# Graph attention and gated experts on one Trainium2 core: the softmax by one exponential with the true row maximum, and the gate's running sum on VectorE

## The chip, the core and the metric

The kernel runs on one core of one Trainium2 chip. The time is device time in microseconds (us), the median of the runs; lower is better. Everything is computed in float32, in matmuls either as float32 or as a sum of products of rounded halves.

## What is computed

Two layers in one kernel over 128 graphs of 128 nodes with 256 features. The first is graph attention; the second is a set of 8 expert networks (two hidden layers with batch norm and relu, one output layer), added up with a gate. Cut to what matters:

```python
# attention, on h = layernorm(x)
Wh = h @ W
e = s1[:, :, None] + s2[:, None, :]            # s1 = Wh @ a1, s2 = Wh @ a2
e = where(e > 0, e, 0.2 * e) + log(adj + 1e-6)
x = x + softmax(e, axis=-1) @ Wh
# experts, on x' = layernorm(x)
feat = mean(x', axis=0)                         # over the 128 graphs
w = softmax(feat @ Wr + br)                     # the gate, one row per node
x = x + sum over experts of w * (relu(bn(relu(bn(x' @ W1)) @ W2)) @ Wo + bo)
```

The logarithm is never taken: the kernel forms exp(leaky(s1+s2) - m) * (adj + 1e-6) and divides by the row's sum. Any m that is constant along a row gives the same softmax.

## The kernel before

The kernel has two blocks, one after the other. The first works through the attention, four graphs at a time (a group): G = 32 groups, tiles of 128 partitions (nodes) by GB = 4 graphs by 128 or 256 columns. Between the blocks the x after attention (x1) goes through DRAM. The second block runs the 8 experts over the 32 groups (tiles).

In the first block all engines run the same step function 34 times and more, each in its own instruction order, tied by semaphores. In step g, SyncE and the engines work at several groups at once: `ago(g, n)` is the group n steps back. In one step:

- TensorE (PE) first transposes p_sb of the group b = g-2 (`ps_pT`, L757), then broadcasts s2 of the group a = g-1 into `ps_s` (L765), then projects the first half of group g (L745), multiplies p by Wh for b (L784), projects the second half, and transposes the normalised x of g+1 (L797) once VectorE has read `ps_h` (the two share PSUM).
- VectorE (DVE), for a: row maximum of s2 out of `ps_s` (`s2max`, L620), three small steps on 128x4 tiles to the two biases of the exponentials (`neg_u` L623, `neg_m` L628, `exp_bias` L634 and L635), with the four statistics instructions of x of g+2 between them (L584). Since s1 + max(s2) bounds the row, the maximum needs only s2. Then the reciprocal of the row sums (L660), the aggregation of the statistics of g+2 (L598) and of x1 of g-3 (L603), x1 of b = PSUM times reciprocal plus residual (L676, four instructions), then for a the larger of the two exponentials (`e_max`, L687), times adjacency (`p_sb`, L694), the row sum (L701), and between them and behind them the statistics of x1 of b (L592, four).
- ScalarE (ACT): copies pT (L524), scales x1 of g-4, graphs 0 and 1, by its 1/std (`x1s_low`, L531), normalises x of g+1 (L514, four), takes two exponentials for each graph of a, of s1+s2 and of 0.2*(s1+s2) (L544 and L546, eight in all; exp of the leaky relu is the larger of them), then a rounding of expert weights (L558 or L562) and the copies of Wh (L567) and of the transposed x (L571).
- GpSimd (POOL): 1/std of x for g+2 by a power (L405 to L412), the sum of the gate over graphs 0 and 1 of g-4 (`acc[:, :HB]`, in the memory of `resb`, L444), the mean and 1/std of x1 of g-3 (L452 to L456), scaling (L462) and summing (L466) of graphs 2 and 3 of g-3, then the preparation of expert weights: in 16 steps either four sums (L472 to L479) or `wq_lo` (L484), in the next 8 `w_lo` (L489).

`acc` holds the sum over groups of x1/std, from which the gate's `feat` comes in the second block. The last two groups are added by `add_group` (L179): four instructions on DVE, x1 times a column of 1/std plus acc, 128x256 each.

The step for group a in DVE's order can't begin before `ps_s` is there, and `ps_s` stands in PE's queue behind the transposes of `p_sb` of the step before.

Of the kernel before, what the change touches and what calls it, by code (L numbers as in the profile page):

```python
# [38 lines left out]
def adj_ffn(nc, x, adj, gnn_w, gnn_a, wr, br, w1, b1, g1, be1, m1, v1, w2, b2, g2, be2, m2, v2, wo, bo, out):  # L39
# [17 lines left out]
    with ExitStack() as ctx:  # L57
# [3 lines left out]
        def sem(name, stack=ctx):  # L61
            return stack.enter_context(nc.semaphore(name))
# [122 lines left out]
        with ExitStack() as sa:  # L185
            def sba(name, shape, dt=F32):
                return sb(name, shape, dt, sa)
# [24 lines left out]
            s2max = sba("s2max", [P, GB])  # L212
            neg_u = sba("neg_u", [P, GB])
            neg_m = sba("neg_m", [P, GB])
            exp_bias = [sba(f"exp_bias{i}", [P, 2, GB]) for i in range(2)]
            e_sb = sba("e_sb", [P, 2, GB, N])
            e_max = sba("e_max", [P, GB, N])
# [7 lines left out]
            x1s_low = sba("x1s_low", [P, HB, D])  # L225
            x1s_high = sba("x1s_high", [P, HB, D])
# [38 lines left out]
            s2max_done = sem("s2max_done", sa)  # L265
            neg_u_done = sem("neg_u_done", sa)
            neg_m_done = sem("neg_m_done", sa)
            bias_done = sem("bias_done", sa)
            e_max_done = sem("e_max_done", sa)
# [13 lines left out]
            x1s_low_done = sem("x1s_low_done", sa)  # L283
            x1s_high_done = sem("x1s_high_done", sa)
            acc_low_done = sem("acc_low_done", sa)
            acc_high_done = sem("acc_high_done", sa)
# [6 lines left out]
            def num(g):  # L293
                return 2 * g[0] + g[1]
# [93 lines left out]
            def _(pool):  # L388
# [5 lines left out]
                nc.gpsimd.memset(acc[:, :, :], 0.0)  # L394
# [38 lines left out]
                def step(g, layer):  # L433
# [5 lines left out]
                    h = ago(g, 4)  # L439
                    if exists(h):  # L440

                        pool.wait_ge(x1s_low_done, num(h) + 1)
                        wait(pool, acc_low_done, num(h))
                        nc.gpsimd.tensor_tensor(acc[:, :HB, :], acc[:, :HB, :], x1s_low[:, :, :],  # L444
                                                ALU.add).then_inc(acc_low_done, 1)
                    t = ago(g, 3)
                    if exists(t) and not is_step(t, G - 1):

                        p = t[1]
                        pool.wait_ge(stats2_done, num(t) + 1)  # L450
                        wait(pool, rstd2_done, num(t))
                        nc.gpsimd.tensor_tensor(mean_all[:, num(t), :], mv2[p][:, :, 0], ones_cols[:, :], ALU.mult)  # L452
                        nc.gpsimd.tensor_tensor(ve2[:, :], mv2[p][:, :, 1], eps_cols[:, :],
                                                ALU.add).then_inc(ve2_done, 1)
                        pool.wait_ge(ve2_done, num(t) + 1)
                        nc.gpsimd.tensor_tensor(rstd_all[:, num(t), :], ve2[:, :], minus_half[:, 0:GB],  # L456
                                                ALU.pow).then_inc(rstd2_done, 1)
                        pool.wait_ge(rstd2_done, num(t) + 1)
                    if exists(t) and not is_step(t, G - 2) and not is_step(t, G - 1):

                        wait(pool, acc_high_done, num(t))
                        nc.gpsimd.tensor_tensor(x1s_high[:, :, :], x1[p][:, HB:, :],  # L462
                                                rstd_all[:, num(t), HB:, None].to_broadcast([P, HB, D]),
                                                ALU.mult).then_inc(x1s_high_done, 1)
                        pool.wait_ge(x1s_high_done, num(t) + 1)
                        nc.gpsimd.tensor_tensor(acc[:, HB:, :], acc[:, HB:, :], x1s_high[:, :, :],  # L466
                                                ALU.add).then_inc(acc_high_done, 1)
# [31 lines left out]
            def _(act):  # L499
# [18 lines left out]
                def step(g, layer):  # L518
# [6 lines left out]
                    t = ago(g, 4)  # L525
                    if exists(t):

                        act.wait_ge(rstd2_done, num(t) + 1)
                        wait(act, acc_low_done, num(t))
                        for b4 in range(HB):  # L530
                            last = nc.scalar.activation(x1s_low[:, b4, :], x1[t[1]][:, b4, :], ACT.Copy,  # L531
                                                        scale=rstd_all[:, num(t), b4:b4 + 1])
                        last.then_inc(x1s_low_done, 1)
# [3 lines left out]
                    a = ago(g, 1)  # L537
                    if exists(a):
                        r = a[1]
                        act.wait_ge(bias_done, num(a) + 1)  # L540
                        wait(act, e_max_done, num(a))

                        for b4 in range(GB):
                            nc.scalar.activation(e_sb[:, 0, b4, :], ps_s[:, b4, :], ACT.Exp,  # L544
                                                 bias=exp_bias[r][:, 0, b4:b4 + 1])
                            last = nc.scalar.activation(e_sb[:, 1, b4, :], ps_s[:, b4, :], ACT.Exp,  # L546
                                                        bias=exp_bias[r][:, 1, b4:b4 + 1], scale=SLOPE)
                        last.then_inc(e_done, 1)
# [29 lines left out]
            def _(dve):  # L578
# [27 lines left out]
                def step(g, layer):  # L606
# [10 lines left out]
                    if exists(a):  # L617

                        dve.wait_ge(s2b_ready, num(a) + 1)
                        nc.vector.tensor_reduce(s2max[:, :], ps_s[:, :, :], AX_X, ALU.max).then_inc(s2max_done, 1)  # L620
                        stats_part(0)
                        dve.wait_ge(s2max_done, num(a) + 1)
                        nc.vector.scalar_tensor_tensor(out=neg_u[:, :], in0=s2max[:, :], scalar=-1.0,  # L623
                                                       in1=wh[r][:, :, D], op0=ALU.mult,
                                                       op1=ALU.subtract).then_inc(neg_u_done, 1)
                        stats_part(1)
                        dve.wait_ge(neg_u_done, num(a) + 1)
                        nc.vector.scalar_tensor_tensor(out=neg_m[:, :], in0=neg_u[:, :], scalar=SLOPE,  # L628
                                                       in1=neg_u[:, :], op0=ALU.mult,
                                                       op1=ALU.min).then_inc(neg_m_done, 1)  # L630
                        stats_part(2)
                        dve.wait_ge(neg_m_done, num(a) + 1)
                        wait(dve, e_done, num(a) - 1)
                        nc.vector.tensor_tensor(exp_bias[r][:, 0, :], wh[r][:, :, D], neg_m[:, :], ALU.add)  # L634
                        nc.vector.scalar_tensor_tensor(out=exp_bias[r][:, 1, :], in0=wh[r][:, :, D], scalar=SLOPE,  # L635
                                                       in1=neg_m[:, :], op0=ALU.mult,
                                                       op1=ALU.add).then_inc(bias_done, 1)
                        stats_part(3)
                    else:
                        for b4 in range(GB):  # L640
                            stats_part(b4)
                    if is_step(g, G - 1):
                        dve.wait_ge(rstd2_done, 1)
                        tile_normalise(dve, 0, range(HB))
                        tile_normalise(dve, 0, range(HB, GB))
# [3 lines left out]

# [15 lines left out]
                    if exists(b):  # L665
# [5 lines left out]
                        wait(dve, x1s_low_done, num(b) - 1)  # L671
                        wait(dve, x1s_high_done, num(b) - 1)
# [10 lines left out]
                    if exists(a):  # L683
# [3 lines left out]
                        nc.vector.tensor_tensor(e_max[:, :, :], e_sb[:, 0, :, :], e_sb[:, 1, :, :],  # L687
                                                ALU.max).then_inc(e_max_done, 1)
                        if with_stats:
                            stats_2(b, 0)  # L690
                        dve.wait_ge(e_max_done, num(a) + 1)
# [3 lines left out]
                                                       in1=e_max[:, :, :], op0=ALU.add,  # L695
# [22 lines left out]
                dve.wait_ge(acc_low_done, G - 2)  # L718
                dve.wait_ge(acc_high_done, G - 2)
# [4 lines left out]
            def _(pe):  # L724
# [24 lines left out]
                def step(g, layer):  # L749
# [9 lines left out]
                    if exists(a):  # L759

                        pe.wait_ge(wh_copied, num(a) + 1)
                        wait(pe, e_done, num(a))
                        wait(pe, s2max_done, num(a))
# [537 lines left out]
```

## Time and profile before

| | us |
|---|---|
| median of 3 runs | 2500.86 |
| lowest, highest run | 2500.14, 2605.57 |
| the profiled execution | 2498.69 |
| its span | 2496.9 |
| busy in the span: PE, DVE, ACT, POOL | 2395.4, 1758.3, 1657.6, 520.9 |

The profiled execution is one of its own; its span is the time between the first and the last instruction. The row of busy tenths in 40 slices (62.4 us each) shows two parts: up to about 340 us DVE is at 9 tenths and PE at 7, and from about 400 us PE is at 9 and DVE at 6. In a row of the timeline, the first column is the start in us from the span's start, the second how long the instruction (or the merged run of xN instructions) lasted. An instruction's duration holds some 0.08 us that the next one on the same engine overlaps, so the pace is read from start to start.

### The profile page before, as it was taken

Reading aid. Unit: us, or ns where it says so; the run is one execution under the profiler, and the core shown is the slowest. Engines: PE = TensorE matmul, PEld = TensorE weight load, DVE = VectorE, ACT = ScalarE, POOL = GpSimd, SP = SyncE. Lnnn points to the kernel's source line nnn. Section 1 sums busy time; section 2 is a strip of 40 time slices with the busy share of each in tenths; the row PEclk is TensorE's granted clock in tenths of the full one; section 3 lists DMA queues with packets and bytes.
Section 4 is the critical chain, followed back from the end, with each engine's and each line's share of the span. In section 5 each row is a group of like instructions: output and inputs, shape, how many; then the busy total and the mean of one; then the engine's idle time right before and its main releaser. Section 6 shows DMA issues by size and latency. Waiting matters only on the chain.

```text
span 2496.9 us, 45276 instructions
## 1 busy us (share of the span) xinstructions
PE 2395.4 (96%) x16304; PEld 2208.3 (88%) x16304; DVE 1758.3 (70%) x2512; ACT 1657.6 (66%) x2526; POOL 520.9 (21%) x548
## 2 busy tenths in 40 slices
PE   7877769999999999999999999999999999999999
PEld 6666658999999999999999999999999999999998
DVE  6999966666666666666666666666666666666665
ACT  6777746666666666666666666666666666666665
POOL 5888852111111100110111111111111101110110
PEclk9999989999999999999999999999999999999999
DMA  5666620000000000000000000000000000000000
GB/s 183 197 191 193 199 95 26 27 26 25 25 25 25 25 25 25 23 19 18 15 25 25 25 25 25 25 25 25 25 25 25 25 25 25 22 20 18 16 18 26
DMA packets 91178, 116.16 MB, mean 47 GB/s; under 512 B 4700, under 2 KB 78856, under 8 KB 91144
## 3 DMA queue, kind: packets, MB, share of 16 engines
q1 hardware_dynamic: 91144, 115.73, 14.4%
q8 instruction: 19, 0.31, 0.1%
q14 instruction: 15, 0.12, 0.0%
HBM read 82.16 MB, written 33.55 MB: 46 GB/s over the span
## 4 chain that ended last, share of the span: by engine, by line
PE 84%; DVE 1%; ACT 0%; issue 0%; ACTq 0%; DVEq 0%
PE ps_y L1201 29%; PE ps_wide L171 29%; PE ps_wide L1183 26%; PE ps_t L132 1%; DVE h_lo L1088 0%; PE ps_y L1249 0%; DVE h L1095 0%; DVE z L1081 0%; ACT h_hi L990 0%; DVE x1t L124 0%; DVE feat_sum L1121 0%; ACT v L995 0%; DVE resb L179 0%; DVE z L1071 0%; DVE h_lo L1103 0%
## 5 line engine op out<-in xcount | busy, mean ns | idle before, releaser
L995 ACT ACTIVATE v<-ps_wide,bn_cols 128x256 f32<-128x256 f32 x768 | 434.3, 565 | 398.8 <-PE ps_wide L1183 271.5
L1003 ACT ACTIVATE h<-ps_wide,bn_cols 128x512 f32<-128x512 f32 x512 | 399.1, 780 | 327.3 <-PE ps_wide L171 327.2
L1201 PE MATMUL ps_y<-wo_lo,h_hi 128*128 128x256 f32 x2048 | 578.8, 283 | 0.0
L1201 PE MATMUL ps_y<-wo_hi,h_hi 128*128 128x256 f32 x2048 | 577.1, 282 | 1.6 <-DVE h_lo L1103 1.6
L1201 PE MATMUL ps_y<-wo_hi,h_lo 128*128 128x256 f32 x2048 | 578.3, 282 | 0.0
L1183 PE MATMUL ps_wide<-xq_hi,wq_hi 128*128 128x256 f32 x1792 | 505.5, 282 | 15.4 <-PEq L185 9.9
L1183 PE MATMUL ps_wide<-xq_lo,wq_hi 128*128 128x256 f32 x1792 | 509.2, 284 | 0.0
L1183 PE MATMUL ps_wide<-xq_hi,wq_lo 128*128 128x256 f32 x1792 | 506.6, 283 | 0.0
L1103 DVE TENSOR_TENSOR h_lo<-h,h_hi 128x1024 fp32r<-128x1024 f32 x256 | 318.3, 1243 | 242.2 <-ACT h_hi L1009 242.2
L1081 DVE SCALAR_TENSOR_TENSOR z<-ps_wide,bn_cols,v 128x512 f32<-128x512 f32 x256 | 192.4, 752 | 318.1 <-PE ps_wide L1183 318.1
L171 PE MATMUL ps_wide<-h_hi,w_hi 128*128 128x512 f32 x1024 | 404.0, 395 | 2.1 <-DVE h_lo L1088 2.1
L171 PE MATMUL ps_wide<-h_lo,w_hi 128*128 128x512 f32 x1024 | 405.7, 396 | 0.0
L171 PE MATMUL ps_wide<-h_hi,w_lo 128*128 128x512 f32 x1024 | 405.6, 396 | 0.0
L973 POOL TENSOR_TENSOR resb<-resb,bias_out 128x1024 f32<-128x1024 f32 x32 | 84.2, 2633 | 1535.8 <-DMA resb<-x_scratch 1535.8
L1088 DVE SCALAR_TENSOR_TENSOR h_lo<-z,h_hi 128x1024 fp32r<-128x1024 f32 x256 | 315.8, 1233 | 117.8 <-ACT h_hi L990 117.7
L1201 PEld LDWEIGHTS ps_y<-wo_hi,h_hi 128*128 128x128 f32 x2048 | 386.5, 189 | 1.9 <-DVE h_lo L1103 1.8
L1201 PEld LDWEIGHTS ps_y<-wo_hi,h_lo 128*128 128x128 f32 x2048 | 387.3, 189 | 0.0
L1201 PEld LDWEIGHTS ps_y<-wo_lo,h_hi 128*128 128x128 f32 x2048 | 386.4, 189 | 0.0
L1183 PEld LDWEIGHTS ps_wide<-xq_hi,wq_hi 128*128 128x128 f32 x1792 | 340.6, 190 | 28.0 <-issue 10.7
L1183 PEld LDWEIGHTS ps_wide<-xq_hi,wq_lo 128*128 128x128 f32 x1792 | 337.9, 189 | 10.0
L1183 PEld LDWEIGHTS ps_wide<-xq_lo,wq_hi 128*128 128x128 f32 x1792 | 339.5, 189 | 0.0
L1095 DVE TENSOR_TENSOR h<-h,w_bc 128x1024 f32<-128x1024 f32 x256 | 313.3, 1224 | 7.8 <-ACT w_bc L1037 4.9
(136 smaller groups left out, 3270.7 us busy)
## 6 DMA issues: line engine op xcount, KB each, us to landing
x_sb<-in_x SPq DMA_DIRECT2D x32, 512.0 KB, 3.5
res<-in_x SPq DMA_DIRECT2D x32, 512.0 KB, 4.5
x1t<-x_scratch SPq DMA_DIRECT2D x32, 512.0 KB, 3.3
resb<-x_scratch SPq DMA_DIRECT2D x32, 512.0 KB, 3.3
out<-resb SPq DMA_DIRECT2D x32, 512.0 KB, 3.0
adj_sb<-in_adj SPq DMA_DIRECT2D x32, 256.0 KB, 3.9
x_scratch<-h SPq DMA_DIRECT2D x16, 512.0 KB, 3.5
x_scratch<-w_bc SPq DMA_DIRECT2D x16, 512.0 KB, 3.0
```

The source lines that it names most:

```text
L132: last = nc.tensor.transpose(ps_x[:, c, b4 * N:(b4 + 1) * N], x1t[:, b4, c * P:(c + 1) * P], ident[:, :])
L171: mm = nc.tensor.matmul(acc_ps, w[:, i, c, cols], s[:, c, :], start=start and n == 0, stop=stop and n == len(terms) - 1)
L973: nc.gpsimd.tensor_tensor(resb[:, :, :], resb[:, :, :], bias_out[:, None, :].to_broadcast([P, GB, D]), ALU.add).then_inc(resb_done, 1)
L995: nc.scalar.activation(v[:, slot, :], ps_l1[:, 0, 0:H], ACT.Identity, bias=bn_cols[:, 1, cols], scale=bn_cols[:, 0, cols]).then_inc(done, 1)
L1003: nc.scalar.activation(h2[:, m, :], ps_l2[:, m, :], ACT.Relu, bias=bn_cols[:, 3, cols], scale=bn_cols[:, 2, cols]).then_inc(r2_done, 1)
L1081: nc.vector.scalar_tensor_tensor(out=z[:, 0, :], in0=ps_l1[:, 1, :], scalar=bn_cols[:, 0, C * e:C * e + 1], in1=v[:, 0:2, :].rearrange("p ...
L1088: nc.vector.scalar_tensor_tensor(out=h1_lo[:, :, :], in0=z[:, :, :], scalar=0.0, in1=h1_hi[:, :, :].bitcast(F32), op0=ALU.max, op1=ALU.sub ...
L1095: nc.vector.tensor_tensor(h2w[:, :, :].rearrange("p c (b n) -> p (c b) n", n=N), h2[:, :, :].rearrange("p c (b n) -> p (c b) n", n=N), w_b ...
L1103: nc.vector.tensor_tensor(h2_lo[p][:, :, :], h2w[:, :, :], h2_hi[p][:, :, :].bitcast(F32), ALU.subtract).then_inc(lo2_done, 1)
L1183: mm = nc.tensor.matmul(out_ps, w[:, e, q, :], x[:, q, :], start=start and n == 0, stop=stop and n == len(terms) - 1, skip_group_check=True)
L1201: mm = nc.tensor.matmul(ps_y[:, b4, :], h[:, c, cols], w[:, e, c, :], start=(e == 0 and k == 0 and b4 % per_bank == 0), stop=(e == E - 1 a ...
```

## The change

For each group the leaky relu is now computed itself. ScalarE writes s1+s2 from PSUM to SBUF (`s_sb`, Identity with s1 as bias, four instructions); DVE takes the larger of it and 0.2 times it (`l_sb`, one scalar_tensor_tensor 128x512) and its negated row maximum (`neg_m`, one reduction 128x512); ScalarE takes one exponential for each graph (four instead of eight), with `neg_m` as bias; `p_sb` reads it directly. `s2max`, `neg_u`, `exp_bias` and `e_max` are gone.

The gate's sum moves: the scaling on ScalarE (two instructions) and the scaling and both sums on GpSimd are gone; DVE does scale and add in four instructions, 128x256 each, for the group g-4, ahead of the reciprocal. The copy of the mean (`mean_all`) goes from GpSimd to ScalarE.

```diff
@@ GpSimd, step
-                    h = ago(g, 4)
-                        nc.gpsimd.tensor_tensor(acc[:, :HB, :], acc[:, :HB, :], x1s_low[:, :, :], ALU.add)
...
-                        nc.gpsimd.tensor_tensor(mean_all[:, num(t), :], mv2[p][:, :, 0], ones_cols[:, :], ALU.mult)
...
-                        nc.gpsimd.tensor_tensor(x1s_high[:, :, :], x1[p][:, HB:, :], rstd_all[...], ALU.mult)
-                        nc.gpsimd.tensor_tensor(acc[:, HB:, :], acc[:, HB:, :], x1s_high[:, :, :], ALU.add)
@@ ScalarE, step, behind the copy of pT
-                    t = ago(g, 4)
-                        for b4 in range(HB):
-                            last = nc.scalar.activation(x1s_low[:, b4, :], x1[t[1]][:, b4, :], ACT.Copy, scale=...)
+                    a = ago(g, 1)
+                        act.wait_ge(s2b_ready, num(a) + 1)
+                        for b4 in range(GB):
+                            last = nc.scalar.activation(s_sb[:, b4, :], ps_s[:, b4, :], ACT.Identity,
+                                                        bias=wh[r][:, b4, D:D + 1])
+                    t = ago(g, 3)
+                        nc.scalar.activation(mean_all[:, num(t), :], mv2[t[1]][:, :, 0], ACT.Copy)
@@ ScalarE, behind normalise(nxt)
-                        act.wait_ge(bias_done, num(a) + 1)
+                        act.wait_ge(neg_m_done, num(a) + 1)
                         for b4 in range(GB):
-                            nc.scalar.activation(e_sb[:, 0, b4, :], ps_s[:, b4, :], ACT.Exp, bias=...)
-                            last = nc.scalar.activation(e_sb[:, 1, b4, :], ps_s[:, b4, :], ACT.Exp, bias=..., scale=SLOPE)
+                            last = nc.scalar.activation(e_sb[:, b4, :], l_sb[:, b4, :], ACT.Exp,
+                                                        bias=neg_m[:, b4:b4 + 1])
@@ DVE, step
-                        (s2max, stats 0, neg_u, stats 1, neg_m, stats 2, exp_bias twice, stats 3)
+                        stats_part(0)
+                        stats_part(1)
+                        dve.wait_ge(s_done, num(a) + 1)
+                        nc.vector.scalar_tensor_tensor(out=l_sb[:, :, :], in0=s_sb[:, :, :], scalar=SLOPE,
+                                                       in1=s_sb[:, :, :], op0=ALU.mult, op1=ALU.max)
+                        stats_part(2)
+                        dve.wait_ge(l_done, num(a) + 1)
+                        nc.vector.tensor_reduce(neg_m[:, :], l_sb[:, :, :], AX_X, ALU.max, negate=True)
                         stats_part(3)
+                    h = ago(g, 4)
+                        for b4 in range(GB):
+                            last = nc.vector.scalar_tensor_tensor(out=acc[:, b4, :], in0=x1[h[1]][:, b4, :],
+                                                                  scalar=rstd_all[:, num(h), b4:b4 + 1],
+                                                                  in1=acc[:, b4, :], op0=ALU.mult, op1=ALU.add)
...
-                        nc.vector.tensor_tensor(e_max[:, :, :], e_sb[:, 0, :, :], e_sb[:, 1, :, :], ALU.max)
```

## Rows read from the trace of the kernel before

**Rows 1.** Busy time by stretch; after the width: PE, PEld, DVE, ACT, POOL, granted clock, DMA share, GB/s
```profile
90.00:110.00 20.00, 17.02 (x83) 14.59 (x83) 17.56 (x54) 15.17 (x34) 18.30 (x25) 0.83 0.63 197
110.00:230.00 120.00, 91.57 (x514) 76.61 (x513) 118.86 (x345) 93.06 (x206) 105.84 (x149) 1.00 0.63 195
...
310.00:350.00 40.00, 24.40 (x120) 20.61 (x120) 32.41 (x87) 19.73 (x49) 27.39 (x32) 0.86 0.33 109
...
400.00:2400.00 2000.00, 1999.19 (x14034) 1867.16 (x14033) 1355.90 (x1481) 1323.60 (x1846) 229.31 (x155) 1.00 0.07 23
```

**Rows 2.** Groups of DVE's, then POOL's instructions, 53 to 309 us: count | busy us, mean ns
```profile
L694 DVE SCALAR_TENSOR_TENSOR p_sb<-adj_sb,e_max 128x512 f32<-128x512 f32 x26 | 37.2, 1430 | 0.0
L628 DVE SCALAR_TENSOR_TENSOR neg_m<-neg_u 128x4 f32<-128x4 f32 x25 | 23.4, 934 | 0.0
...
L634 DVE TENSOR_TENSOR exp_bias<-wh,neg_m 128x4 f32<-128x4 f32 x25 | 20.9, 834 | 0.0
...
L701 DVE TENSOR_REDUCE rowsum<-p_sb 128x4 f32<-128x512 f32 x25 | 16.6, 663 | 0.0
...
L484 POOL TENSOR_TENSOR wq_lo<-w_stage,wq_hi 128x896 f32 x8 | 16.7, 2088 | 0.0
```

**Rows 3.** Timeline of DVE, one step with little work on POOL
```profile
39.48 0.69 DVE L620 TENSOR_REDUCE s2max<-ps_s 128x4 f32<-128x512 f32 x1
40.09 0.42 DVE L584 BATCH_NORM_STATS2 st<-x_sb 128x6 f32<-128x256 f32 x1
...
41.23 0.15 DVE L634 TENSOR_TENSOR exp_bias<-wh,neg_m 128x4 f32<-128x4 f32 x1
...
42.44 1.62 DVE L676 SCALAR_TENSOR_TENSOR w_bc<-ps_th,rinv,res 128x256 f32<-128x256 f32 x4
43.99 0.68 DVE L687 TENSOR_TENSOR e_max<-e_sb 128x512 f32<-128x512 f32 x1
44.59 0.42 DVE L592 BATCH_NORM_STATS2 st<-w_bc 128x6 f32<-128x256 f32 x1
44.92 0.67 DVE L694 SCALAR_TENSOR_TENSOR p_sb<-adj_sb,e_max 128x512 f32<-128x512 f32 x1
...
47.24 0.69 DVE L620 TENSOR_REDUCE s2max<-ps_s 128x4 f32<-128x512 f32 x1
```

**Rows 4.** Timeline of all engines, DVE and POOL in the middle of the stage
```profile
152.77 1.66 DVE L676 SCALAR_TENSOR_TENSOR h<-ps_th,rinv,res 128x256 f32<-128x256 f32 x4
...
154.36 1.80 POOL L444 TENSOR_TENSOR resb<-resb,x1s_low 128x512 f32<-128x512 f32 x1
...
155.28 1.42 DVE L694 SCALAR_TENSOR_TENSOR p_sb<-adj_sb,e_max 128x512 f32<-128x512 f32 x1
...
162.97 1.02 POOL L409 TENSOR_TENSOR rstd<-ve,minus_half 128x4 f32<-128x4 f32 x1
...
163.73 0.68 DVE L687 TENSOR_TENSOR e_max<-e_sb 128x512 f32<-128x512 f32 x1
```

**Rows 5.** The same timeline, PE and ACT
```profile
156.76 0.66 PE L757 MATMUL ps_pT<-ident,p_sb 128*128 128x128 f32 x4 [1.61 <-DVE p_sb L694]
...
157.25 1.06 PE L765 MATMUL ps_s<-ident,wh 128*128 128x128 f32 x8
...
161.22 0.37 ACT L544 ACTIVATE e_sb<-ps_s,exp_bias 128x128 f32<-128x128 f32 x1
161.49 0.36 ACT L546 ACTIVATE e_sb<-ps_s,exp_bias 128x128 f32<-128x128 f32 x1
```

**Rows 6.** Timeline of DVE behind the last step: the sum for one of the last groups
```profile
350.77 1.64 DVE L179 SCALAR_TENSOR_TENSOR resb<-h,rstd_all,resb 128x256 f32<-128x256 f32 x4
```

**Rows 7.** Timeline of DVE: p_sb of groups 3, 28 and 31
```profile
53.29 1.42 DVE L694 SCALAR_TENSOR_TENSOR p_sb<-adj_sb,e_max 128x512 f32<-128x512 f32 x1
...
308.97 1.42 DVE L694 SCALAR_TENSOR_TENSOR p_sb<-adj_sb,e_max 128x512 f32<-128x512 f32 x1
...
336.50 1.41 DVE L694 SCALAR_TENSOR_TENSOR p_sb<-adj_sb,e_max 128x512 f32<-128x512 f32 x1
```

More of the change, by code:

```diff
@@ L211, in adj_ffn @@
             wh = [sba(f"wh{i}", [P, GB, D + 2]) for i in range(2)]
-            s2max = sba("s2max", [P, GB])
-            neg_u = sba("neg_u", [P, GB])
             neg_m = sba("neg_m", [P, GB])
-            exp_bias = [sba(f"exp_bias{i}", [P, 2, GB]) for i in range(2)]
-            e_sb = sba("e_sb", [P, 2, GB, N])
-            e_max = sba("e_max", [P, GB, N])
+            s_sb = sba("s_sb", [P, GB, N])
+            l_sb = sba("l_sb", [P, GB, N])
+            e_sb = sba("e_sb", [P, GB, N])
             p_sb = sba("p_sb", [P, GB, N])
@@ L524, in step @@
                         nc.scalar.activation(pT[:, :, :], ps_pT[:, :, :], ACT.Copy).then_inc(pT_copied, 1)
-                    t = ago(g, 4)
-                    if exists(t):
-                        act.wait_ge(rstd2_done, num(t) + 1)
-                        wait(act, acc_low_done, num(t))
-                        for b4 in range(HB):
-                            last = nc.scalar.activation(x1s_low[:, b4, :], x1[t[1]][:, b4, :], ACT.Copy,
-                                                        scale=rstd_all[:, num(t), b4:b4 + 1])
-                        last.then_inc(x1s_low_done, 1)
+                    a = ago(g, 1)
+                    if exists(a):
+                        r = a[1]
+                        act.wait_ge(s2b_ready, num(a) + 1)
+                        wait(act, l_done, num(a))
+                        for b4 in range(GB):
+                            last = nc.scalar.activation(s_sb[:, b4, :], ps_s[:, b4, :], ACT.Identity,
+                                                        bias=wh[r][:, b4, D:D + 1])
+                        last.then_inc(s_done, 1)
+                    t = ago(g, 3)
+                    if exists(t) and not is_step(t, G - 1):
+                        act.wait_ge(stats2_done, num(t) + 1)
+                        nc.scalar.activation(mean_all[:, num(t), :], mv2[t[1]][:, :, 0],
+                                             ACT.Copy).then_inc(mean2_done, 1)
                     nxt = ago(g, -1)
@@ L536, in step @@
                         normalise(nxt)
-                    a = ago(g, 1)
                     if exists(a):
-                        r = a[1]
-                        act.wait_ge(bias_done, num(a) + 1)
-                        wait(act, e_max_done, num(a))
+                        act.wait_ge(neg_m_done, num(a) + 1)
+                        wait(act, p_done, num(a))
                         for b4 in range(GB):
[L544 to L547, printed above, removed]
+                            last = nc.scalar.activation(e_sb[:, b4, :], l_sb[:, b4, :], ACT.Exp,
+                                                        bias=neg_m[:, b4:b4 + 1])
                         last.then_inc(e_done, 1)
@@ L617, in step @@
                     if exists(a):
-                        dve.wait_ge(s2b_ready, num(a) + 1)
-                        nc.vector.tensor_reduce(s2max[:, :], ps_s[:, :, :], AX_X, ALU.max).then_inc(s2max_done, 1)
                         stats_part(0)
[L622 to L625, printed above, removed]
                         stats_part(1)
[L627 to L630, printed above, removed]
-                        stats_part(2)
[L632 to L637, printed above, removed]
+                        dve.wait_ge(s_done, num(a) + 1)
+                        wait(dve, e_done, num(a))
+                        nc.vector.scalar_tensor_tensor(out=l_sb[:, :, :], in0=s_sb[:, :, :], scalar=SLOPE,
+                                                       in1=s_sb[:, :, :], op0=ALU.mult,
+                                                       op1=ALU.max).then_inc(l_done, 1)
+                        stats_part(2)
+                        dve.wait_ge(l_done, num(a) + 1)
+                        nc.vector.tensor_reduce(neg_m[:, :], l_sb[:, :, :], AX_X, ALU.max,
+                                                negate=True).then_inc(neg_m_done, 1)
                         stats_part(3)
@@ L648, in step @@
                     t = ago(g, 3)
+                    h = ago(g, 4)
+                    if exists(h) and not is_step(h, G - 2) and not is_step(h, G - 1):
+                        dve.wait_ge(rstd2_done, num(h) + 1)
+                        dve.wait_ge(acc_step, num(h) + 1)
+                        dve.wait_ge(mean2_done, num(h) + 1)
+                        for b4 in range(GB):
+                            last = nc.vector.scalar_tensor_tensor(out=acc[:, b4, :], in0=x1[h[1]][:, b4, :],
+                                                                  scalar=rstd_all[:, num(h), b4:b4 + 1],
+                                                                  in1=acc[:, b4, :], op0=ALU.mult, op1=ALU.add)
+                        last.then_inc(acc_step, 1)
                     if exists(nxt):
@@ L761, in step @@
                         pe.wait_ge(wh_copied, num(a) + 1)
-                        wait(pe, e_done, num(a))
-                        wait(pe, s2max_done, num(a))
+                        wait(pe, s_done, num(a))
                         for b4 in range(GB):
```

40 lines of the change are left out of this document (8 added, 32 removed).

## The prediction

> **What bounds the kernel now.** I read the busy time by stretch first. From 400 to 2400 us PE is busy for 1999 of 2000 us, and the change touches nothing there. In the attention stage (110 to 230 us) DVE is busy 118.9 of 120 us, PE 91.6, ACT 93.1, POOL 105.8 [rows 1]. So the stage runs at DVE's pace, and the change can move only its share: `p_sb` of group 3 starts at 53.29 us and that of group 28, 25 steps later, at 308.97, which is 10.23 us per step [rows 7].
>
> Busy is not the same as working, so I read the groups of DVE instructions next, for durations that don't fit the tile. `neg_m` and the first `exp_bias` work on 128x4 and last 0.93 and 0.83 us on average [rows 2]; in an early step, where POOL has little to do, the same form lasts 0.15 [rows 3]. `p_sb` lasts 1.43 on average and 0.67 in the early step [rows 2, 3]. The timeline of both engines tells why. POOL's sum L444 lasts from 154.36 to 156.16 and `p_sb`, begun at 155.28, ends at 156.70, 0.54 us after it, which is about its own length [rows 4]. Statistics, row sums and x1 (one SBUF tensor, or one and PSUM) show no such stretch. So a DVE instruction with two SBUF inputs waits while POOL's sum runs. Per step this costs (1.43-0.67) + (0.93-0.15) + (0.83-0.15) = 2.2 us, and the remaining small part sits in `neg_u`. The early step takes 47.24-39.48 = 7.76 us [rows 3]; with 2.2 this makes 9.96 of the 10.23, so the account of a step closes to 0.3 us.
>
> **The change, part by part, per step of DVE** (paces from start to start in the early step, or duration less the 0.08 us overlap [rows 3]).
> - Gone: `s2max` 0.61, `e_max` 0.60, four instructions on 128x4 at 0.07 = 0.28. Sum 1.49.
> - New: `l_sb`, two SBUF inputs and 512 columns like `p_sb`: 0.59. The reduction of `l_sb` is of `rowsum`'s form: 0.663-0.08 = 0.58 [rows 2]. The sum of the gate: four instructions exactly like L179, whose four last 1.64, so 1.56 [rows 6]. Sum 2.73.
> - DVE's own work per step then is 7.76 - 1.49 + 2.73 = 9.00 us. More than before by 1.24, where the waits on POOL gave 2.2 to win.
> - The waits. POOL loses L444, L452, L462 and L466. What is left are the power chains (L405 to L412, L453 to L456) and one piece of weight work. I place them in the new step below.
>
> **The loop that then sets the pace.** DVE gets a new wait, `s_done`, and the sum isn't all. From the start of `p_sb`: 0.67 for itself, 0.06 to PE, transposes and `ps_s` from 156.76 to 158.31, 1.55 [rows 5], then ACT's four `s_sb`. They read PSUM with a bias as the exponentials do, whose starts are 0.25 to 0.27 apart and which last 0.37 [rows 5]: 3 x 0.25 + 0.38 = 1.13, and 0.04 for each of two hand-overs. So `l_sb` starts 0.67+0.06+1.55+1.13+0.08 = 3.49 us after `p_sb`. DVE gets there on its own after `p_sb` 0.59, row sum 0.58, five statistics 5 x 0.34, and 0.12 at the step's turn, 2.99. It idles 0.5 us. The rest of the step: `l_sb` 0.59, statistics 0.34, reduction 0.58, statistics 0.34, turn 0.12, sum of the gate 1.56, reciprocal and aggregations 0.61 (from 41.23 to 42.44, less 0.14 for the two biases, 0.34 and 0.12), x1 1.55 and statistics 0.34 [rows 3, 6] = 6.03. The step is 3.49 + 6.03 = 9.52 us, against 10.23.
>
> **What lies beside it.** The four exponentials follow `neg_m` (1.5 us behind `l_sb`) and `normalise`, and end about 3.3 us behind `l_sb`; `p_sb` needs them at 6.0, so 2.7 us cover them. If that cover went, ACT would set the pace. ACT trades four exponentials for four `s_sb` and loses `x1s_low`. PE needs x1 to be read before L797; `p_sb` follows that by one statistics and its own length, as before. The move of `normalise` behind `s_sb` makes SyncE's load of x two groups on later by about 1 us; it still lands some 2 us before its statistics are due. The sum reads x1 of g-4 before x1 of g-2 overwrites it in the same order on one engine, and its 1/std is a step old: neither waits.
>
> POOL's weight work in the new step starts behind the second power, near the end of `p_sb`, and is over 2 to 3 us later (L484, the longest, lasts 2.09 [rows 2]), just as `l_sb` begins; it meets only row sum and statistics, which don't wait. The sum of the gate falls where POOL is idle. A tie remains: behind the first chain POOL goes on at 154.36, so the second power, with a 128x4 addition of some 0.3 us ahead of it, starts at about 154.7; `p_sb`, without `e_max` ahead of it, would start at 152.77 + 1.55 + 0.34 = 154.66 [rows 3, 4]. Does a power hold DVE up? `e_max` starts 0.76 us into a power and lasts its plain 0.68 [rows 4]. So not in its last quarter; how it is in the first part no row shows. The bounds for the cost of the tie are 0 and 0.95 us per step. I take about 0, as the nearest row has it, and keep 0.95 for the range.
>
> The Trainium skill (SBUF — State Buffer, what follows "Reading the diagram") says that DVE instructions with two SBUF inputs and GpSimd instructions take the shared port pair as an exclusive lock, and that the first one has it for the whole instruction. The trace agrees for the sums: `p_sb` 1.42 against 0.67. It does not for the power's last 0.26 us, during which `e_max` ran undelayed. By the page the tie could cost its full 0.95; by the row, nothing.
>
> **The sum.** 25 steps x (9.52 - 10.23) = -17.7 us. Ahead of group 3 the sum of the gate is new in a step in which POOL was hardly in the way, and `s_sb` delays the others by 0.2: +1.1. One step at about 95 us ran in part at the lower clock (granted 0.83 from 90 to 110 us [rows 1]); there the new loop leads through PE, where DVE's had slack: +0.9. Behind group 28, three steps last 336.50-308.97 = 27.5 now; without the statistics of x I work them out as 8.8, 10.2 (with 1.39 for the normalising of the first tile) and 9.9 (at a granted clock of 0.86 [rows 1] PE's part grows by 1.15) = 28.9: +1.4. The sum for g-4 in the last step stands ahead of an aggregation that POOL's sums wait for, against L444 gone: +0.2. Total -14.1 us. On the profiled execution this gives a span of 2496.9 - 14.1 = 2483; the median lies 2.2 us above the profiled execution's time, so I forecast 2500.9 - 14.1 = 2487 us.
>
> **The rivals.**
> 1. *The power blocks `p_sb`.* POOL's second power starts a few hundredths before `p_sb` and keeps it out to its end: 0.95 us x 25 = +24, to 2511, slower than before. For it: the start times tie. Against it: `e_max` beside a power. It decides as soon as the power is first and holds the port for over 0.55 us (14.1/25).
> 2. *The new loop is shorter than I make it*, and DVE's work alone sets the pace: 9.00 instead of 9.52, -13 us, 2474. For it: nothing but that my hand-overs are upper ones; against it: each link stands in a row.
> 3. *The stage gives back nothing or much more*, through a transfer or a clock that I don't see: under 2450 the step would have to last 8.2 us, less than DVE's own 9.00; over 2551 it would have to last 12.0.
>
> **How the numbers follow.** The forecast's own range is 2480 to 2497, at 0.62; rival 1 gets 0.20, rival 2 0.12, the rest 0.06. From 2474 (rival 2) to 2511 (rival 1) the range leaves out 1 to 2 in 10. Two per cent, about what a measurement of this kernel can tell from no change, are 50 us: neither rival reaches them. Within 2%: 0.96; faster 0.01, slower 0.03.
>
> **What would show it.** In the changed kernel's profile `p_sb` should last 0.67 to 0.7 and no DVE instruction on 128x4 more than 0.2; `l_sb` should have some 0.5 us of idle time before it in each step, released by ACT's `s_sb`; the sum of the gate should take 1.6 us per step with POOL idle beside it; the starts of `p_sb` should be 9.5 us apart; the sums of POOL's busy time should fall by some 140 us; the stretch from 400 us on should be unchanged but for its place. `p_sb` at 1.3 to 1.6 with a power on POOL beside it would show rival 1, a step of 9.0 without idle time rival 2. An idle time before `p_sb`, released by the exponentials, would break the account of ACT, and durations of the gate's sum over 0.48 us each the account of the port.

## The result and the profile after

The changed kernel takes 2566.3 us (median; 2562.9 to 2568.1) against 2500.1 for the kernel before: 1.0264 times as long, 95% interval 1.0251 to 1.0277. The run of 2605.57 us in the table of times before is in the slow state that a program sometimes shows and is left out; the other five lie between 2498.7 and 2500.9. The forecast was 2487, with a range from 2474 to 2511; the change makes the kernel slower by 66 us, beyond rival 1, and only the remainder of 0.06 (rival 3) held such a time.

The page's line of busy times of the kernel after (engine, busy us, share of the span, instructions):

```profile
PE 2429.2 (95%) x16304; PEld 2239.4 (87%) x16304; DVE 1731.1 (68%) x2504; ACT 1639.7 (64%) x2497; POOL 390.0 (15%) x427
```

Busy time by stretch of the kernel after, columns as in [rows 1]:

```profile
110.00:230.00 120.00, 90.02 (x426) 75.93 (x425) 86.96 (x283) 68.01 (x156) 44.98 (x78) 0.88 0.49 159
...
460.00:2460.00 2000.00, 1999.18 (x14038) 1867.90 (x14038) 1355.77 (x1479) 1324.08 (x1848) 233.54 (x157) 1.00 0.07 24
```

The second stage is as before, 1999 of 2000 us of PE [rows 1]. In the first, DVE is busy for 87 of 120 us where it was 119, and POOL for 45 instead of 106: the work is gone as planned, and the engines idle. TensorE's granted clock is 0.88 instead of 1.00. POOL's total fell by 131 us and ACT's by 18.

The timeline of the kernel after through one step, from `p_sb` back to what it waited for (in brackets the idle time before an instruction and its releaser):

```profile
151.98 1.65 DVE L624 SCALAR_TENSOR_TENSOR resb<-h,rstd_all,resb 128x256 f32<-128x256 f32 x4
...
153.90 0.35 DVE L579 BATCH_NORM_AGGREGATE mv<-st 128x2 f32<-128x6 f32 x4
...
154.17 1.63 DVE L652 SCALAR_TENSOR_TENSOR h<-ps_th,rinv,res 128x256 f32<-128x256 f32 x4
...
154.39 0.21 ACT L512 ACTIVATE mean_all<-mv 128x4 f32 x1 [4.40 <-DVE mv L579]
...
154.57 2.08 ACT L489 ACTIVATE xn<-x_sb,nb,rstd 128x256 f32<-128x256 f32 x4
...
156.55 1.26 ACT L522 ACTIVATE e_sb<-l_sb,neg_m 128x128 f32<-128x128 f32 x4
...
156.70 1.10 PE L768 MATMUL ps_th<-ident,xn 128*128 128x128 f32 x8 [2.36 <-ACT xn L489]
...
157.85 0.43 DVE L568 BATCH_NORM_STATS2 st<-h 128x6 f32<-128x256 f32 x1 [2.05 <-ACT e_sb L522]
...
158.19 0.67 DVE L667 SCALAR_TENSOR_TENSOR p_sb<-adj_sb,e_sb 128x512 f32<-128x512 f32 x1
...
169.73 0.67 DVE L667 SCALAR_TENSOR_TENSOR p_sb<-adj_sb,e_sb 128x512 f32<-128x512 f32 x1
```

Read it from the bottom. `p_sb` lasts 0.67, the waits on POOL of [rows 2, 4] are gone. But DVE idled 2.05 us for the exponentials. Those could not begin before the normalising, and that stood behind a copy of 512 numbers, `mean_all`, on which ScalarE waited 4.40 us. The copy needs `mv2` of group g-3, which DVE aggregates in this same step, behind the four instructions of the gate's sum. This closes a loop: aggregation, copy, normalising (2.1), exponentials (1.3), `p_sb`, transposes, `ps_s`, `s_sb`, `l_sb`, maximum, sum, aggregation. It takes 169.73-158.19 = 11.54 us. Before, the same copy was POOL's, which had nothing urgent behind it.

Between 60 and 330 us the view of waits puts it together (who waited for whom: us in total, times, longest):

```profile
ACT mean_all L512 <- DVE mv L579: 96.1, 22, 4.7
...
PE ps_th L768 <- ACT xn L489: 46.0, 21, 3.0
DVE st L568 <- ACT e_sb L522: 43.0, 21, 2.3
...
DVE l_sb L599 <- ACT s_sb L506: 22.7, 18, 1.7
```

`p_sb` of group 3 starts at 58.85 us and that of group 28 at 370.45: 12.46 us per step over 25 steps, against 10.23 before [rows 7]. The difference of the spans, 65.1 us, is 56 here, 5.6 ahead of group 3 and 3.6 behind group 28. 12.46 is more than 11.54, because 16 of the 25 steps last 12.7 to 13.0; what these are comes below.

### The profile page after: what moved, and what is told of

Same layout as the page of the kernel before. It is cut to its first block, busy times and chain, and to the rows that moved or that the text cites. A ratio compares the mean times of both kernels' runs of the same rounds, so it can differ in the third digit from the quotient of the medians.

```text
span 2562.0 us, 45072 instructions
## 1 busy us (share of the span) xinstructions
PE 2429.2 (95%) x16304; PEld 2239.4 (87%) x16304; DVE 1731.1 (68%) x2504; ACT 1639.7 (64%) x2497; POOL 390.0 (15%) x427
## 4 chain that ended last, share of the span: by engine, by line
PE 83%; DVE 1%; ACT 0%; issue 0%
PE ps_y L1172 28%; PE ps_wide L171 28%; PE ps_wide L1154 25%; PE ps_t L132 1%; DVE h_lo L1059 0%; DVE h L1066 0%; PE ps_y L1220 0%; DVE z L1052 0%; ACT v L966 0%; DVE h_lo L1074 0%; ACT h_hi L980 0%; ACT w_bc L1008 0%; ACT h L974 0%; DVE z L1042 0%; DVE resb L1082 0%
## 5 line engine op out<-in xcount | busy, mean ns | idle before, releaser
L1154 PE MATMUL ps_wide<-xq_hi,wq_hi 128*128 128x256 f32 x1792 | 506.8, 283 | 12.7 <-PEq L185 9.2
```

The source lines that it names most:

```text
L1154: mm = nc.tensor.matmul(out_ps, w[:, e, q, :], x[:, q, :], start=start and n == 0, stop=stop and n == len(terms) - 1, skip_group_check=True)
```

## The experiments

I held three theories against each other. Q: the queue, that is the copy of the mean ahead of the normalising. L: the new softmax is a longer chain (`s_sb`, `l_sb`, maximum, exponential) and costs this whatever stands in the queue. C: the lower clock has another cause and is what costs.

### The copy behind the exponentials

```diff
@@ ScalarE, step
-                    t = ago(g, 3)
-                    if exists(t) and not is_step(t, G - 1):
-                        act.wait_ge(stats2_done, num(t) + 1)
-                        nc.scalar.activation(mean_all[:, num(t), :], mv2[t[1]][:, :, 0],
-                                             ACT.Copy).then_inc(mean2_done, 1)
                     (normalise, four exponentials)
+                    (the same five lines)
```

> The changed kernel with one block moved: ScalarE's copy of the mean (mean_all, with its wait for DVE's aggregation) stands behind the four exponentials instead of ahead of the normalising. Same instructions, same work. Theory Q (queue): in the changed kernel the copy waits 4.3 us per step for an aggregation that DVE does late in the same step, and the normalising and the exponentials stand behind it in ScalarE's order, so that DVE waits about 2 us for the exponentials. Then this kernel should come to my forecast: p_sb every 9.5 us where the clock is full, no idle time of DVE behind the exponentials, 2480 to 2500 us. Theory L (longer chain): s_sb, l_sb, maximum and exponential in a row are too long whatever stands in the queue; then no better than 2540. Theory C (clock): the lower granted clock of the changed kernel (0.74 to 0.95 in the stage) comes from something else and is the cause; then the clock stays low and the time above 2530.

Measured: 2494.8 us, 0.9978 of the kernel before (0.9968 to 0.9987). Moving one instruction gives back 71 us; Q holds, L and C as whole causes fall. The timeline of this kernel:

```profile
156.56 1.01 POOL L440 TENSOR_TENSOR rstd_all<-ve,minus_half 128x4 f32 x1 [0.18 <-POOL ve L437]
156.69 0.67 DVE L667 SCALAR_TENSOR_TENSOR p_sb<-adj_sb,e_sb 128x512 f32<-128x512 f32 x1
...
159.00 1.15 ACT L506 ACTIVATE s_sb<-ps_s,wh 128x128 f32<-128x128 f32 x4 [0.30 <-PE ps_s L736]
...
160.18 0.69 DVE L599 SCALAR_TENSOR_TENSOR l_sb<-s_sb 128x512 f32<-128x512 f32 x1 [0.59 <-ACT s_sb L506]
...
161.99 1.27 ACT L517 ACTIVATE e_sb<-l_sb,neg_m 128x128 f32<-128x128 f32 x4
162.04 1.66 DVE L624 SCALAR_TENSOR_TENSOR resb<-w_bc,rstd_all,resb 128x256 f32<-128x256 f32 x4
...
164.23 1.63 DVE L652 SCALAR_TENSOR_TENSOR w_bc<-ps_th,rinv,res 128x256 f32<-128x256 f32 x4
...
164.44 0.20 ACT L523 ACTIVATE mean_all<-mv 128x4 f32 x1 [1.19 <-DVE mv L579]
...
165.22 1.35 PE L768 MATMUL ps_th<-ident,xn 128*128 128x128 f32 x8 [1.04 <-DVE w_bc L652]
...
165.99 0.43 DVE L568 BATCH_NORM_STATS2 st<-w_bc 128x6 f32<-128x256 f32 x1
...
166.34 0.67 DVE L667 SCALAR_TENSOR_TENSOR p_sb<-adj_sb,e_sb 128x512 f32<-128x512 f32 x1
```

This is the step that was forecast. From `p_sb` to `l_sb` 3.49 us, as worked out; the idle time before `l_sb` is 0.59 (0.5 worked out); the exponentials end at 163.26, 2.7 us ahead of the statistics in front of `p_sb`. The step lasts 9.65 instead of 9.52. The largest difference is at one place: from x1 (164.23) to its statistics (165.99) pass 1.76 us, where the forecast had 1.55 from x1 to `e_max` [rows 3]; from `l_sb` to x1 it is 4.05 us instead of 4.14. With `e_max` gone, the instruction behind x1 reads x1, and the kernel has DVE wait for the semaphore `x1_done` there.

Two other things stand in it. Rival 1 is decided: a power begins on POOL at 156.56, `p_sb` 0.13 us later, and `p_sb` lasts its plain 0.67. It is so in all 26 steps from group 3 to group 28: the power begins 0.10 to 0.22 us ahead, and `p_sb` lasts 0.67 or 0.68. And not all steps last 9.65: eight of 25 last 10.6 to 10.9, so that the average is 10.02.

### The copy back on GpSimd

```diff
@@ GpSimd, step, ahead of ve2; the block on ScalarE is gone
+                        nc.gpsimd.tensor_tensor(mean_all[:, num(t), :], mv2[p][:, :, 0], ones_cols[:, :],
+                                                ALU.mult).then_inc(mean2_done, 1)
```

> The changed kernel with the copy of the mean back on GpSimd, ahead of the addition of epsilon, as in the kernel before. Theory Q: the same release as with the copy behind the exponentials, 2480 to 2500 us; GpSimd's second power then starts 0.2 us later, behind the start of p_sb, so p_sb should not wait for it. Theories L and C: above 2530 us.

Measured: 2499.0 us, ratio 0.9997 (0.9987 to 1.0007). The same release by another way; steps of 9.65 again, with more long steps among them than above (the average is 10.17), and a granted clock of 0.93 between 110 and 230 us. The power begins 0.1 us behind `p_sb` in most steps, which lasts 0.67 or 0.68.

### The aggregation earlier, the copy in its place

```diff
@@ DVE, step
-                        (the gate's sum, four instructions)
                     reciprocal
-                    if exists(nxt):
-                        aggregate_1(nxt)
                     if exists(t):
                         aggregate_2(t)
+                        (the gate's sum, four instructions)
+                    if exists(nxt):
+                        aggregate_1(nxt)
```

> The changed kernel with the copy of the mean left where it is on ScalarE, but DVE's aggregation that it waits for moved ahead of the four instructions of the gate's sum (and of the other aggregation), 1.8 us earlier. A dose, not a cure. Theory Q: the loop aggregation, copy, normalising, exponentials, p_sb gets 1.8 us shorter per step, some 30 steps: 45 to 60 us less than the changed kernel, 2505 to 2525 us, with DVE's wait for the exponentials near 0.2 us instead of 2. Theories L and C: no change from 2566, as all instructions and the chain of the softmax are the same.

Measured: 2503.8 us, ratio 1.0014 (1.0004 to 1.0023): 62 us less than the changed kernel. The plain steps last 9.84 instead of 11.54, 1.70 less, and the aggregation starts 2.08 us behind `l_sb` where it was 3.79. Beside them stand eight steps of 10.55 to 10.65: ScalarE rounds expert weights (`wq_hi`, 0.93 us) just as these begin, and in the one from 147.94 us `l_sb` waits 1.00 instead of 0.59 us for `s_sb`. The average is 10.19. The copy's waits, from 60 to 300 us:

```profile
ACT mean_all L512 <- DVE mv L579: 65.5, 24, 3.1
```

ScalarE still waits 2.7 us for each copy, where it was 4.4 in the changed kernel; DVE now waits only 0.2 us for the exponentials, as expected. The run lies 1 us below the expected range. The steps at the lower clock went too, all but one, and I had not counted that: the granted clock between 110 and 230 us is 1.00, with PE busy for 96 of 120 us.

### The wait alone, in the kernel before

```diff
@@ ScalarE, step of the kernel before, behind x1s_low and ahead of normalise(nxt)
+                    t = ago(g, 3)
+                    if exists(t) and not is_step(t, G - 1):
+                        act.wait_ge(stats2_done, num(t) + 1)
+                        nc.scalar.activation(mean_all[:, num(t), :], mv2[t[1]][:, :, 0],
+                                             ACT.Copy).then_inc(mean2_done, 1)
@@ GpSimd: the copy is gone; DVE waits for mean2_done of g-5 ahead of the aggregation
```

> The kernel before with one thing changed: the copy of the mean (128x4) on ScalarE, behind the scaling of x1 and ahead of the normalising, with its wait for DVE's aggregation. Neither softmax nor sum is touched. Theory Q: the copy ends about 3 us later than ScalarE would have begun the normalising, and eight exponentials follow it; less what DVE's waits for GpSimd give back, 2 to 3 us per step, 2550 to 2585 us, with idle time of DVE behind the exponentials. If the wait only hurts together with the new softmax, it is within 10 us of the kernel before.

Measured: 2588.7 us, ratio 1.0353 (1.0336 to 1.0371). One copy of 128x4, moved to ScalarE's queue in the old kernel, costs 89 us; most steps last 13.5 or 13.6 us, 13.36 on average. It is above the expected range by 4 us. The waits from 60 to 300 us:

```profile
ACT mean_all L537 <- DVE mv L608: 61.3, 18, 3.6
DVE e_max L695 <- ACT e_sb L551: 49.5, 19, 2.9
```

So the cost needs neither the new softmax nor the sum on DVE. It is larger here by some 17 us. Eight exponentials instead of four stand behind the copy, which fits, but no run separates this from the waits on POOL and the clock (0.89 from 110 to 230 us).

### Each part alone

The sum on DVE, with the softmax as before and the copy on GpSimd (all edits of the diff that concern `acc`, none of the others):

> The kernel before with the gate's sum alone moved to DVE (four instructions); two exponentials, their maximum and the copy of the mean on GpSimd stay as before. DVE's work is 7.76 + 1.56 = 9.3 us per step with the waits on GpSimd's sums gone, against 10.2 in the kernel before: by theory Q and by my sum of the forecast 0.9 x 25 less, 2475 to 2485 us. If moving the sum is itself what costs (its port or its waits), it is above 2500.

The softmax alone, with sum and copy as before:

> The kernel before with the softmax alone changed (s_sb, l_sb, true maximum, four exponentials); the gate's sum stays on ScalarE and GpSimd and the copy of the mean on GpSimd. No wait for the aggregation stands in ScalarE's queue. Theory Q: DVE's own step is 7.4 us, the loop through p_sb, transposes, ps_s, s_sb about 8.1, and l_sb and p_sb each wait up to 0.8 us for GpSimd's sums: 9 to 9.7 us per step, 2475 to 2495 us. Theory L (the chain of the new softmax itself costs the time): above 2530 us, as in the changed kernel.

Measured: the sum alone 2478.2 us, 0.9921 (0.9904 to 0.9937); the softmax alone 2491.0 us, 0.9961 (0.9947 to 0.9975). Each is a gain. With the sum alone the steps last 9.20, where 9.32 were worked out, and in the stretch in which POOL prepares `wq` 9.46 and 9.65. With the softmax alone `p_sb` still meets POOL's sums (it lasts 1.15 to 1.35 in most steps). The steps last 9.4 to 10.2 and five of them 11.0 to 12.0, each of these with a stretch of lower clock in it; on average they last 10.17, so the time came out in the expected range but the step, expected at 9 to 9.7, did not. Theory L is refuted a second time.

### The long steps: PE kept busy

Eight of 25 steps in the kernel with the copy behind the exponentials, and 16 of 25 in the changed kernel, are 0.9 to 1.5 us longer than the others. In the changed kernel, at such a step:

```profile
171.37 1.92 PE L736 MATMUL ps_s<-ident,wh 128*128 128x128 f32 x8
...
173.32 1.14 ACT L506 ACTIVATE s_sb<-ps_s,wh 128x128 f32<-128x128 f32 x4 [0.83 <-PE ps_s L736]
```

`ps_s` takes 1.92 us instead of 1.06 [rows 5]: TensorE runs at 1.2 instead of 2.4 GHz. It had idled for 2.55 us for the normalised x and then for 1.13 us for `p_sb`. The transposes and `ps_s` lie on the loop, so the lower clock costs there directly. To tell whether the idling or something else lowers the clock, PE does part of the projection twice, in the place where it idles:

```diff
@@ PE, step, in the kernel with the copy behind the exponentials
                     if exists(g):
+                        project(g, range(GB // 2, GB))
                         project(g, range(GB // 2, GB)).then_inc(wh_ready, 1)
```

> The kernel with the mean behind the exponentials, and PE does the projection of graphs 2 and 3 of each group twice (four 128x258 matmuls more per step, 0.96 us at the full clock, the same result), in a place where it otherwise waits about 1 us for DVE to read ps_h. It tells what the steps of 10.7 us beside those of 9.65 are. If they come from the granted clock, which in that kernel falls to one half for 3.4 us about every second step after PE has idled there, the clock should stay at 1.00 and all steps last 9.65 to 9.75: 8 to 10 us less than without the fill, 2485 to 2488 us. If they come from GpSimd or DMA, the fill changes nothing or costs up to 1 us per step.

Measured: 2493.1 us, ratio 0.9971 (0.9960 to 0.9982). Busy time by stretch, first without the repetition:

```profile
110.00:230.00 120.00, 102.63 (x535) 84.40 (x534) 107.72 (x350) 90.61 (x200) 56.12 (x102) 0.96 0.63 196
```

and with it:

```profile
110.00:230.00 120.00, 116.26 (x643) 101.51 (x642) 110.20 (x356) 92.08 (x209) 56.61 (x103) 1.00 0.66 205
```

The four matmuls take 1.74 us, and not 0.96 as I had written: the graphs 2 and 3 done twice take 161.40 to 164.88 us, 3.48, in this trace. PE is busy for 116 instead of 103 us, the clock stays at 1.00, and every step from group 3 to group 28 lasts 9.65 or 9.75: 9.69 on average against 10.02, 8 us over 25 steps as expected. The whole gained only 2, which is not clear of noise (the intervals of the two ratios overlap), and lies above the expected range: ahead of group 3 the extra matmuls cost 4 us, and the rest lies within what single runs of the kernel without the repetition differ by (2491.5 to 2498.9). So the repetition is a test and no remedy.

The same in the changed kernel itself, with the projection done three times:

> The changed kernel as it is, with the copy of the mean in its place, and PE does the projection of graphs 2 and 3 of each group three times instead of once (eight 128x258 matmuls more per step, 1.9 us at the full clock, the same result), where it idles 2.4 to 3 us for the normalised x. It measures what part of the loss is the granted clock. The steps of the changed kernel last 11.55 us where the clock is at 1.00 and up to 12.95 where it falls, 12.46 on average. If the fall of the clock follows from PE's idling, the clock stays at 1.00 here and every step lasts 11.5 to 11.7: (12.46 - 11.6) x 25 = 20 us and a few more behind group 28 less, 2538 to 2550 us; the other 40 to 45 us of the loss are the wait itself. If the clock falls for another reason, the fill makes the low stretches longer: 2570 us or more.

Measured: 2556.6 us, ratio 1.0222 (1.0205 to 1.0239), 10 us less than the changed kernel and 6 above the expected range.

```profile
110.00:230.00 120.00, 114.98 (x612) 99.29 (x612) 92.52 (x304) 74.00 (x169) 50.62 (x89) 1.00 0.51 164
```

The clock is at 1.00 for the whole stage. The 25 steps from group 3 on (68.19 to 361.40 us) last 11.73 us on average instead of 12.46, 18 us less; ahead of them the extra matmuls cost 9, which I had not counted. Up to 256 us the steps last mostly 11.55 and 11.99 in turn, and most steps of the changed kernel at the full clock last 11.55 or 11.98 too. So the matmuls themselves, some 3.5 us of work per step and not 1.9, hardly lengthen them. Per step, then, 0.73 us of the loss is the clock, and the fall goes away in both kernels when PE's idle time is filled. The Trainium skill (TensorE: Matmul & The Clock Gate, "HAM oscillation — how this bites in real kernels") describes a clock that falls again in every round of a loop because PE waits in every round, there for DMA. The runs agree that such waits can bring the clock down, with another engine as what is waited for, and in 16 of 25 rounds instead of in each.

How much PE waits doesn't tell by itself whether the clock falls. PE's waits from 110 to 230 us (us in total, times, longest), in the kernel before, where the clock was 1.00:

```profile
PE ps_pT L757 <- DVE p_sb L694: 20.3, 12, 1.8
PE ps_th L797 <- DVE h L676: 7.8, 6, 1.3
```

and in the kernel with the copy behind the exponentials, where it was 0.96:

```profile
PE ps_pT L729 <- DVE p_sb L667: 5.9, 12, 0.5
PE ps_th L768 <- DVE w_bc L652: 5.9, 6, 1.0
PE ps_th L768 <- DVE h L652: 4.7, 6, 1.1
```

28.1 us of waiting left the clock up, and 16.5 did not. The kernel with the aggregation earlier (22.5 us, 1.00) is a second such case. What sets them apart stays open.

### The copy at the end, the sum in two halves

```diff
@@ ScalarE: the copy of the mean at the end of the step, behind xnT
@@ DVE, step
                         stats_part(1)
+                        (wait for rstd, mean and the last sum of h; the gate's sum for graphs 0 and 1)
                         dve.wait_ge(s_done, num(a) + 1)
                         (l_sb, statistics, maximum, statistics)
-                        (the gate's sum, four instructions)
+                        (the gate's sum for graphs 2 and 3)
```

> An attempt to beat both kernels: the changed kernel with the copy of the mean at the end of ScalarE's step, and two of the four instructions of the gate's sum ahead of l_sb, where DVE idles about 0.6 us for s_sb. Same work. Theory Q with DVE's own work of 9.0 to 9.1 us as the next bound: steps of 9.1 us where the clock is full, 0.5 x 25 us less than with the mean behind the exponentials alone, 2475 to 2485 us. If the idle time before l_sb is not on the loop (the aggregation, x1 or PE is), no gain over 2495.

Measured: 2468.0 us, ratio 0.9871 (0.9854 to 0.9887). 32 us less than the kernel before and 98 less than the changed one, with the same instructions as the changed one. It also lies 7 us below the expected range.

```profile
110.00:230.00 120.00, 107.23 (x590) 87.96 (x589) 118.29 (x385) 100.09 (x224) 61.12 (x110) 1.00 0.71 220
```

DVE is busy for 118 of 120 us again, as in the kernel before [rows 1], now without waits on POOL in it: the steps last 8.97 and 9.11, DVE's own 9.0 of the forecast. The clock stays at 1.00 with no matmul added. PE waits less in each step (11.9 us from 110 to 230, against 16.5); that this is why isn't shown, as the kernel before waits more and keeps the clock.

## Why the prediction was wrong

- *What bounds the kernel* held: the second stage didn't move, the first is set step by step.
- *DVE's own work per step* held: 9.00 worked out, 8.97 to 9.11 where nothing else is in the way. So did the reading of [rows 2, 4], that DVE's instructions with two SBUF inputs waited for POOL: `p_sb` is 0.67 to 0.69 in all kernels without POOL's sums. The gate's sum lasts 1.65, like L179 [rows 6].
- *The loop over `s_sb`* held: 3.49 from `p_sb` to `l_sb` as worked out. One term was off, x1 to statistics, 1.76 for 1.55, 0.2 us: DVE's wait on the semaphore of its own x1, which `e_max` had covered.
- *What lies beside it* is the step that failed. It lists for ScalarE four exponentials against four `s_sb` and `x1s_low` gone. The copy of the mean, which the diff puts ahead of `normalise` with a wait for `stats2_done`, is in no sum of the prediction (the cut of the diff shows the copy without its wait). I hadn't asked when what it waits for happens, nor what stands behind it in ScalarE's order. Rows of the trace before hold the answer. By the prediction's own terms the aggregation ends 1.85 + 0.12 + 1.56 + 0.61 = 4.14 us behind `l_sb`. The copy of 0.2 us, the normalising and the exponentials (1.13 in the prediction) come behind it, and the normalising is this row:

```profile
159.06 2.06 ACT L514 ACTIVATE xn<-x_sb,nb,rstd 128x256 f32<-128x256 f32 x4
```

So the exponentials end 4.14 + 0.2 + 2.06 + 1.13 = 7.5 us behind `l_sb` and not 3.3. `p_sb` was due at 6.0 with 0.34 of statistics in front of it: a wait of 1.8 us and a step of 11.4. Measured: 2.05 and 11.54; the exponentials took 1.26.
- *The clock.* The prediction gave it one step at the lower level, 0.9 us, and 1.15 us behind group 28. In the changed kernel it falls in 16 of 25 steps: another 0.73 us per step, of which nothing stood in the sum. Even the step as forecast has it, 0.33 per step (10.02 against 9.69), 8 us in all; with the copy out of the way the kernel takes 2494.8 us, still 8 above the forecast, and this is the largest part of that. The missing question was what TensorE's share of the loop costs at the lower level.
- Per step the account is: 9.52 forecast, +0.17 for what the forecast step lacked (9.69 on average at the full clock, most of it x1 to statistics), +2.04 for the copy (11.73 at the full clock against 9.69), +0.73 for the clock = 12.46, as measured.
- *Rival 1* named the right place for a loss beyond the forecast, `p_sb`, with the wrong cause. The tie came true, with the power 0.10 to 0.22 us ahead in the kernel with the copy behind the exponentials, and the power didn't hold `p_sb`. Of the rule of the Trainium skill (SBUF — State Buffer, "Reading the diagram") that a GpSimd instruction has the shared port for its whole length, the runs confirm the case of the 128x512 sums and not that of the power: here the measurement decides. *Rival 2*, 2474 with DVE's own work as the bound, is what the last kernel reaches by filling the gap before `l_sb`.
- *Rival 3* dismissed a step above 12.0 us as out of reach. It was passed (12.46) by a mechanism that the rivals didn't contain, since they were drawn from the instructions that cost time and not from the waits that the diff adds. Its two bounds are also a little off: by the prediction's own sum 2450 us would need a step of 8.05 us and 2551 one of 12.09, not 8.2 and 12.0; nothing hangs on it.
- *SyncE's load of x* was said to land some 2 us before its statistics are due. In the changed kernel, where the normalising comes late, DVE waits 0.44 us for it at 160.89; the wait is just covered, since `s_sb` ends at 161.65.

## What to carry to other kernels

In a diff that moves work between engines in a hand-written order, list the waits, not only the instructions: for each one ask in which place of the producer's step its condition comes true, and what is queued behind it. A copy of 0.2 us cost 71 us in one place of a queue; eight instructions later, behind the normalising and the exponentials, nothing waited for it. Where the chain that sets a step leads through TensorE, and TensorE waits in each step, price its part at the lower clock as well.

## What the runs showed of the hardware

- A GpSimd power on 128x4, 1.01 us long and begun 0.10 to 0.22 us ahead, didn't delay a DVE instruction with two SBUF inputs (0.67 or 0.68 us in 26 of 26 steps); a GpSimd sum of 128x512 did, by 0.76 us on average [rows 2, 3]. The other way round, a power that begins some 0.1 us behind `p_sb` lasts 1.38 to 1.49 instead of 1.01 (kernel with the aggregation earlier).
- TensorE's waits of 1.0 us for x1 and 0.5 us for `p_sb` in each step went with a clock that fell to 1.2 GHz in eight of 25 steps (0.96 from 110 to 230 us). Filled with matmuls, or at steps of 9.0 us, it stayed at 1.00. But it also stayed there in the kernel before, whose waits for `p_sb` last up to 1.8 us and for x1 up to 1.3, so that the length of the waits doesn't settle it.
- On DVE an instruction that reads what the one before it has written, behind the semaphore wait that this kernel puts there, starts some 0.2 us later than an independent one (1.76 against 1.55 us behind the start of four instructions of 128x256).
